# A two-block vision tower with a mixture of experts: slack in the order table, and ScalarE's squares in the last layer norm

## The reference, cut to what matters

```python
h = tok(x)                                   # gated projection
h = layernorm(h + attention_window(h))       # block 0, 16 heads, window of 64 each side
h = layernorm(h + quantised_mlp(h))          # block 0, the "quantised layer"
h = layernorm(h + attention_causal(h))       # block 1, 16 heads
h = layernorm(h + experts(h))                # block 1, 8 experts, top 2

# quantised_mlp: every input row is scaled to +-127 and rounded, weights to -1, 0, 1
act_quant(x) = clip(round(x * s), -128, 127) / s,  s = 127 / max|x|
g = act_quant(x) @ Wg ; u = act_quant(x) @ Wu
out = act_quant(square(relu(g)) * u) @ Wd

# experts: routing, capacity, two matmuls per expert, then a norm of its own
scores = softmax(x @ wg); gates, idx = top_k(scores, 2)
loc = cumsum(masks) - 1 + offsets;  keep = loc < C
y = layernorm(h + moe) * gamma + beta        # first norm of the end
out = layernorm(h + y)                       # second norm of the end
```

## Time and profile before

| | |
|---|---|
| median of 3 runs | 1016.46 us (1016.39 to 1018.25) |
| the profiled execution, its own time | 1015.96 us |
| its span, first to last instruction | 1014.1 us |
| first stage / experts / end | 0 to about 674 / to about 977 / to 1014.1 us |
| TensorE busy | 856.6 us (84%) |
| VectorE busy | 543.6 us (54%) |
| ScalarE busy | 415.4 us (41%) |
| GpSimd busy | 305.7 us (30%) |
| mean granted TensorE clock | 0.918 of full |

### The profile page before, as it was taken

The page is one execution under the profiler, slowest core; times in us unless marked ns, Lnnn a source line. Parts: engine busy times, 40 slices in busy tenths (PEclk is TensorE's granted clock), DMA queues, the critical chain, the costliest instruction groups (busy, mean ns, idle before and its releaser), DMA issues. The chain is left out here.

```text
span 1014.1 us, 14085 instructions
## 1 busy us (share of the span) xinstructions
PE 856.6 (84%) x4842; PEld 542.4 (53%) x4842; DVE 543.6 (54%) x2104; ACT 415.4 (41%) x717; POOL 305.7 (30%) x365
## 2 busy tenths in 40 slices
PE   6979999898697798798899798439999999999930
PEld 2655556556355345345445253326777877877820
DVE  1268535798798698788878685510211211210247
ACT  1316345585684576685565455113121021022003
POOL 6104214335244232122252422370213212311332
PEclk9999999899899799899799697659999999999975
DMA  9642202202202202202231300631135135233242
GB/s 347 201 180 65 65 21 64 64 3 64 64 2 64 64 1 64 64 1 64 85 105 33 97 1 26 248 120 42 16 125 141 21 120 141 46 100 68 29 106 83
DMA packets 57510, 81.48 MB, mean 80 GB/s; under 512 B 6624, under 2 KB 51041, under 8 KB 55008
## 3 DMA queue, kind: packets, MB, share of 16 engines
q1 hardware_dynamic: 49520, 70.48, 21.6%
q0 software_dynamic: 7296, 9.47, 5.5%
q10 hardware_dynamic: 624, 0.63, 0.2%
HBM read 35.37 MB, written 19.68 MB: 54 GB/s over the span
## 5 line engine op out<-in xcount | busy, mean ns | idle before, releaser
L1101 DVE CUSTOM_DVE_ANT_0 junk<-ps,maskb 128x256 bf16<-128x256 f32 (+4 forms) x512 | 205.4, 434 | 66.9 <-PE ps L820 63.1
L646 ACT ACTIVATE probs<-ps 128x512 f32<-128x512 f32 (+1 forms) x304 | 157.5, 551 | 93.1 <-PE ps L843 86.5
L1553 PE MATMUL ps<-dxT,qs 128*128 128x320 f32 x512 | 141.4, 437 | 1.3 <-DVE dxT L1617 1.3
L1565 PE MATMUL ps<-ks,hTe 128*128 128x256 f32 x640 | 139.3, 379 | 0.0
L1587 ACT ACTIVATE hTe<-ps,qs 128x640 f32<-128x640 f32 x64 | 50.8, 794 | 204.6 <-PE ps L1553 204.5
L1509 POOL DMA_INDIRECT mixed_rows<-ysb,ids x40 | 61.7, 1544 | 228.3 <-DVE ysb L1637 225.4
L1565 PEld LDWEIGHTS ps<-ks,hTe 128*128 128x128 f32 x640 | 121.1, 190 | 16.3
L843 PE MATMUL ps<-qs,ks 99*128 99x256 bf16 (+4 forms) x512 | 107.8, 298 | 21.4 <-DVE nmax L1101 8.8
L1553 PEld LDWEIGHTS ps<-dxT,qs 128*128 128x128 f32 x512 | 98.1, 192 | 42.6 <-DVE dxT L1617 1.9
L820 PE MATMUL ps<-ks,qs 96*128 96x256 bf16 (+4 forms) x512 | 107.8, 295 | 11.2 <-DVE nmax L1101 7.4
L859 PE MATMUL ps<-probs,vaug 128*32 128x256 f32 (+4 forms) x1024 | 93.7, 440 | 5.7 <-issue 4.2
(11 more groups left out here) (179 smaller groups left out, 1184.3 us busy)
## 6 DMA issues: line engine op xcount, KB each, us to landing
qs<-parts SPq DMA_DIRECT2D x96, 128.0 KB, 2.4
ks<-parts SPq DMA_DIRECT2D x96, 128.0 KB, 2.4
qs<-w SPq DMA_DIRECT2D x8, 1024.0 KB
ks<-w SPq DMA_DIRECT2D x8, 1024.0 KB, 4.9
dispatched_rows<-att SPq DMA_DIRECT2D x8, 650.0 KB, 10.5
ks<-dispatched_rows SPq DMA_DIRECT2D x4, 650.0 KB, 7.4
x_sb<-xT SPq DMA_DIRECT2D x8, 256.0 KB, 4.0
mixed_rows<-h SPq DMA_DIRECT2D x4, 512.0 KB, 3.6
```

Source lines behind the costliest of these rows:

```text
L646: act.activation(probs_of(u)[:, heads[0]:heads[-1] + 1, :], turned_bank((u, half, i))[:, 0:len(heads) * w].rearrange("p (j n) -> p j n", n=w),
L1101: ins = dve.tensor_tensor_reduce(out=junk[:, b - (b > V_BANK), a * (hi - lo):(a + 1) * (hi - lo)], in0=score_bank((u, half, i))[:, a * (hi ...
L1553: ins = mm(bank(2 * (n % 2) + c)[:, 0:HC], w1s[:, e % 2, k, m * P:(m + 1) * P], dxT[:, e % 2, k, c * HC:(c + 1) * HC], start=(k == 0), sto ...
L1565: ins = mm(bank(4 + n % 2)[:, 0:D], hTe[:, e % 2, m, t * P:(t + 1) * P], w2s[:, e % 2, m, :], start=(m == 0), stop=(m == MH - 1))
```

## The change

Five things are edited.

1. In "ffn" every piece from ScalarE's roundings on moves back by one: L759 from piece 0 to 1, L1278 from 1 to 2, the turn from 4 to 5 and the tiles from 5 to 6. The phase has 28 pieces and starts one step later for every batch. The tiles so stand two steps later than before.
2. In each tile ScalarE's rounding (L771) moves from the tile's step 2 to its step 3. VectorE's subtraction behind it stays in step 4.
3. Attention's norm (L1164) is cut in two: two tiles in piece 5, two in a new piece 6.
4. "route" gets an empty piece between the choice and the count: the count moves from piece 5 to 6, the positions from 6 to 8 to 7 to 9. The gate and route of batch 2 move from steps 249 and 251 to 258 and 260.
5. In the end, for batches 0 to 2, the second norm's statistics leave VectorE. The row sums come as a second output of the instruction that makes the input, a small instruction turns them into minus the mean, and ScalarE squares the centred rows and sums the squares as a second output. Batch 3 keeps the statistics as they were.

```diff
-    ("wq", 2, 20), ... ("o", 0, 54), ("ffn", 0, 60),
-    ("qkv", 3, 66), ("o", 1, 85), ("ffn", 1, 91), ...
+    ("wq", 2, 20), ... ("o", 0, 54), ("ffn", 0, 61),
+    ("qkv", 3, 66), ("o", 1, 85), ("ffn", 1, 92), ...
-    ("o", 6, 245), ("gate", 2, 249), ("route", 2, 251), ("send", 2, 271), ("o", 7, 278), ("gate", 3, 282),
+    ("o", 6, 245), ("gate", 2, 258), ("route", 2, 260), ("send", 2, 271), ("o", 7, 278), ("gate", 3, 282),
-STEPS = {"tok": 12, "qkv": 8, "o": 6, "ffn": 27, "gate": 2, "route": 9, ...}
+STEPS = {"tok": 12, "qkv": 8, "o": 7, "ffn": 28, "gate": 2, "route": 10, ...}
-FQT, FIRST_TILE, PER_TILE = 4, 5, 4
+FQT, FIRST_TILE, PER_TILE = 5, 6, 4
@@ scalar, ffn
-                            if c == 0:
+                            if c == 1:
                                 act.wait_ge(scale_done, i + 1)
...
-                            t = tile_at(c, HIDDEN + 1)
+                            t = tile_at(c, HIDDEN + 2)
                             if t is not None:
                                 act.wait_ge(fh_scaled, NT * i + t + 1)
@@ vector, quant
+                        if c == 2:
                             dve.wait_ge(fq_raised, NT * (i + 1))
@@ vector, o
-                            if c == 5:
-                                normed(0, NT, x, b, ROOTS["o", i])
+                            if c in (5, 6):
+                                normed(2 * (c - 5), 2 * (c - 5) + 2, x, b, ROOTS["o", i])
@@ scalar, the end
+                    def squares(q):
+                        act.wait_ge(mean2_done, q + 1)
+                        for t in range(q * NT, q * NT + NT):
+                            act.activation(n1[:, t, :], xa[:, t, :], ACT.Square, bias=nmean2[:, t:t + 1],
+                                           accum_out=sq2[:, t:t + 1]).then_inc(sq2_done, 1)
+
+                    squares(0)
                     for q in range(B):
-                        act.wait_ge(cbias[1], q + 1)
+                        if q + 1 < LAST:
+                            squares(q + 1)
+                        act.wait_ge(cbias, q + 1)
@@ vector, the end, second(q)
+                                dve.scalar_tensor_tensor(xa[:, t, :], n1[:, t, :], rs[:, 0, t:t + 1], hb(t), ALU.mult,
+                                                         ALU.add, accum_out=sum2[:, t:t + 1]).then_inc(xb_done, 1)
...
+                        if q:
+                            last_bias(q - 1)
+                        if q < LAST:
+                            dve.wait_ge(xb_done, q * NT + NT)
+                            dve.tensor_scalar(nmean2[:, c], sum2[:, c], -1.0 / D, None,
+                                              ALU.mult).then_inc(mean2_done, 1)
+                        else:
+                            stats(1, q)
+                    def variance(q):
+                        dve.wait_ge(sq2_done, q * NT + NT)
+                        dve.tensor_scalar(sq2[:, c], sq2[:, c], 1.0 / D, EPS_LN, ALU.mult, ALU.add).then_inc(cvar[1], 1)
...
                     for q in range(B):
                         if q + 1 < B:
                             begin(q + 1)
+                        if q:
+                            variance(q - 1)
                         second(q)
-                        if q:
-                            last_bias(q - 1)
```

More of the change, by code:

```diff
@@ L98 @@
     ("tok", 0, -20), ("qkv", 0, -8), ("tok", 1, -4), ("bias", 0, 1), ("bias", 1, 2), ("wq", 0, 4), ("wq", 1, 8),
-    ("wq", 2, 20), ("qkv", 1, 14), ("tok", 2, 22), ("tok", 3, 34), ("qkv", 2, 38), ("o", 0, 54), ("ffn", 0, 60),
-    ("qkv", 3, 66), ("o", 1, 85), ("ffn", 1, 91), ("qkv", 4, 98), ("o", 2, 117), ("ffn", 2, 123), ("qkv", 5, 130),
-    ("o", 3, 149), ("ffn", 3, 155), ("qkv", 6, 162), ("o", 4, 181), ("gate", 0, 185), ("route", 0, 187),
+    ("wq", 2, 20), ("qkv", 1, 14), ("tok", 2, 22), ("tok", 3, 34), ("qkv", 2, 38), ("o", 0, 54), ("ffn", 0, 61),
+    ("qkv", 3, 66), ("o", 1, 85), ("ffn", 1, 92), ("qkv", 4, 98), ("o", 2, 117), ("ffn", 2, 124), ("qkv", 5, 130),
+    ("o", 3, 149), ("ffn", 3, 156), ("qkv", 6, 162), ("o", 4, 181), ("gate", 0, 185), ("route", 0, 187),
     ("send", 0, 196), ("qkv", 7, 196), ("o", 5, 213), ("gate", 1, 217), ("route", 1, 219), ("send", 1, 228),
-    ("o", 6, 245), ("gate", 2, 249), ("route", 2, 251), ("send", 2, 271), ("o", 7, 278), ("gate", 3, 282),
+    ("o", 6, 245), ("gate", 2, 258), ("route", 2, 260), ("send", 2, 271), ("o", 7, 278), ("gate", 3, 282),
     ("route", 3, 284), ("send", 3, 293),)
-STEPS = {"tok": 12, "qkv": 8, "o": 6, "ffn": 27, "gate": 2, "route": 9, "send": 4, "bias": 2, "wq": 4}
-FQT, FIRST_TILE, PER_TILE = 4, 5, 4
+STEPS = {"tok": 12, "qkv": 8, "o": 7, "ffn": 28, "gate": 2, "route": 10, "send": 4, "bias": 2, "wq": 4}
+FQT, FIRST_TILE, PER_TILE = 5, 6, 4
 HIDDEN = 1
@@ L318, in build @@
         hb_done, n1_done, xb_done = (sem(n) for n in ("hb_done", "n1_done", "xb_done"))
-        c_stats, cvar, crstd, cbias, fin_done, out_done = (
-            [sem(f"{n}{i}") for i in range(2)] for n in ("c_stats", "cvar", "crstd", "cbias", "fin_done", "out_done"))
+        c_stats, cvar, crstd, fin_done, out_done = (
+            [sem(f"{n}{i}") for i in range(2)] for n in ("c_stats", "cvar", "crstd", "fin_done", "out_done"))
+        cbias, mean2_done, sq2_done = (sem(n) for n in ("cbias", "mean2_done", "sq2_done"))
         y_in = [sem(f"y_in{i}") for i in range(NTT // 2)]
@@ L1027, in dense @@
                                 ins.then_inc(d_full(("gate", i, "lg"))[0], 1)
-                        if phase == "route" and c == 5:
+                        if phase == "route" and c == 6:
                             pe.wait_ge(chosen, i + 1)
@@ L1457, in build @@
             moments2 = sb3("moments2", [P, NTT, 2])
+            sum2 = sb3("sum2", [P, NTT])
+            sq2 = sb3("sq2", [P, NTT])
+            nmean2 = sb3("nmean2", [P, NTT])
             rs = sb3("rs", [P, 2, NTT])
@@ L1678, in last_bias @@
                         dve.wait_ge(crstd[1], q + 1)
-                        dve.scalar_tensor_tensor(nb2[:, c], moments2[:, c, 0], -1.0, rs[:, 1, c], ALU.mult,
-                                                 ALU.mult).then_inc(cbias[1], 1)
+                        if q < LAST:
+                            dve.tensor_tensor(nb2[:, c], nmean2[:, c], rs[:, 1, c], ALU.mult).then_inc(cbias, 1)
+                        else:
+                            dve.scalar_tensor_tensor(nb2[:, c], moments2[:, c, 0], -1.0, rs[:, 1, c], ALU.mult,
+                                                     ALU.mult).then_inc(cbias, 1)
                     dve.wait_ge(hb_done, NTT)
```

30 lines of the change are left out of this document (17 added, 13 removed).

## The result

The changed kernel takes 999.79 us (median of 4 runs, 999.01 to 1000.09) against 1017.11 us for the kernel before beside it (4 runs, 1016.39 to 1018.25): a ratio of 0.9829, 95% interval 0.9805 to 0.9853. The forecast was 1007.0 us with 999 to 1018 around it. Faster was right, and 7 of the 17 us were not foreseen. The profiled execution took 999.01 us with a span of 997.1 us, 17.0 us less than before.

The account below looks back on a forecast made before the run. VectorE was taken to bound layer starts and the end, and with TensorE the quantised tiles. -4.2 - 3.4 - 1.8 = -9.4 us from 1015.96 gives 1006.6, plus 0.5 to the median 1007.0 us; forecast's own range 1002 to 1011, overall 999 to 1018.

Parts of the forecast that it names:

- What bounds the kernel: First stage: TensorE and VectorE both full in the quantised layer's tiles, VectorE alone at layer starts; the end is VectorE's chain.
- part 2: ScalarE's rounding L771 in each tile, one step later: not on the path, 0 us, between -2 and +12.
- Part 1: Roundings and start of the layer: VectorE's wait at L1278, four pieces, goes; -4.2 us, bounds 2.8 to 6.9.
- Part 3: Tiles two steps later: last tiles' statistics and norm move beside the next attention layer's sum; 0 us, between -4 and +7.
- the cut norm: Attention's norm cut in two at the layer's start: a bank comes free 1 us earlier, costed at nothing.
- Part 4: Routes: TensorE's waits around batch 2's route go, positions' delay hidden behind GpSimd's mask; -3.4 us, between -7 and +2.
- Part 5: The end: statistics of batches 0 to 2 leave VectorE, squares go to ScalarE; -1.8 us, between -3.4 and -0.5.
- The signs named ahead: Checks: L1280 under 1.5 us, no TensorE waits around 612 to 620 us, end 1.5 to 2 us shorter, L1707 wait.
- The clock: Rival: shorter stalls at layer starts and batch 2's route leave TensorE at full clock; 998 us, chance 0.16.
- Load, not waits: Rival: VectorE's bursts are only shifted and waits return later; only the end and about 1 us stay; 1013.5 us, chance 0.20.
- The late rounding: Rival: in the tiles L771 comes later and VectorE waits for it over sixteen gaps; 1018.5 us, chance 0.16.
- The squares set the end: Rival: if one ScalarE square takes 1.1 us, the end gives nothing and somewhat more; 1009.5 us, chance 0.06.

Follow-up runs that it names:

- part 4 alone: Kernel before with only batch 2's gate and route at 258 and 260 and the empty piece in every route: 1017.71 us, ratio 0.9989.
- the changed kernel timed again: The changed kernel, unaltered, timed a second time beside the leave-one-out kernels: 998.40 us, ratio 0.9817 to the kernel before.
- the ruler: Kernel before with only the end's edits (squares on ScalarE, accumulator outputs on VectorE), first stage untouched, so its trace serves as comparison there: 1016.42 us, ratio 0.9963.
- one step further: The changed kernel with L771 one step later still, in the step of VectorE's subtraction: 1023.81 us, ratio 1.0079 to the kernel before.

## Why the prediction was right in sign and short in size

- **What bounds the kernel, and part 2 (0 us): wrong, and the step that failed.** "This is not on the path, since VectorE is full in these tiles" rested on one window, 285.6 to 307.2 us, with VectorE at 20.71 of 21.60. Over steps 60 to 184 it is busy 243 of 291 us, and 22.1 of its idle us are at the maxima, waiting for TensorE. The prediction asked what the rounding itself delays (the subtraction, with room), and not what is queued behind the waiting rounding on ScalarE. Queued there was work that empties TensorE's banks (L665 in the tile shown): its waits for ScalarE fall from 20.3 to 6.6 us with part 2. That is worth 8.6 us alone and 14.3 in the changed kernel; the bound of -2 was far off.
- **Part 1 (-4.2):** the wait went as said (4.2 to 0.8), and in the changed kernel it is worth 3.9. Taken alone it is worth nothing that can be measured, and in its trace TensorE's longer busy time at a lower clock takes back the 6.6 us of idle time that it saved; a sum of separate terms could not say this.
- **Part 3 (0), and the cut norm (0, priced within part 1):** nothing can be measured for the cut norm. The later tiles have no run of their own; they are in part 1's, where ScalarE waits 6.3 us more at L771 (26.1 to 32.4).
- **Part 4 (-3.4):** the move gave 5.1, the clock among it; the empty piece took 3.0 where the prediction put nothing. "That wait is hidden behind the mask" was wrong by 0.9 to 1.1 us at GpSimd, and the cast queued behind it came late for VectorE; that this is the whole of the 3.0 is not shown. "The scatter of batch 2 stays at step 271" was true of the order and missed who waits behind it.
- **Part 5 (-1.8):** -3.0, inside its -0.5 to -3.4 and near the end at which both accumulator reads cost nothing. The mechanism was right, the prices too high: 1.98 us for the squares in place of 2.7, and next to nothing in place of 0.08 us for an accumulator output on VectorE.
- **The signs named ahead** came in the main: 0.8 us at L1280, no waits for the maxima's banks around the old 612 to 620 us, 2.14 us at L1707, the experts from 660 us on. The count waits 0.69 us where nothing was expected, the end is 3.0 us shorter and not 1.5 to 2, and the clock's mean is 0.922.
- **The rivals.** The clock did come along at batch 2's route (0.85 to 0.95 with part 4 alone); in the layers it is 0.92 in the profiled execution against 0.94 before, and 0.93 in the changed kernel timed again against 0.92 in the ruler, so the gain there is in the main not the clock's. "Load, not waits" (1013.5, by its own terms 1013.7) fell by the time, though half of its sign came: TensorE's waits for the maxima in steps 60 to 184 went only from 11.2 to 9.2 us, and what fell was its waits for ScalarE. "The late rounding" did not happen, but one step further it does. "The squares set the end" fell: four take 1.98 us (985.38 to 987.36).
- The Trainium skill (ScalarE: Activation LUTs, Rules for kernel authors) would keep adds and multiplies, which a square is, on VectorE. By the same page's figures (What ACT_TABLE_LOAD costs) four squares take an estimated 1.7 us; measured are 1.98 with their accumulator reads. On the price of the instructions this case agrees (1.79 us for four tiles' statistics on VectorE); the gain comes from taking work off the engine whose list is the chain.

Open: how much more the parts of the layer are worth together than apart, and why the clock is granted less with part 1 alone. By the ratios the parts come to -5.8 us apart (-8.6 + 1.7 + 1.1) and to -12.7 together, by the medians to -10.2 and -12.8, and each of these ratios is uncertain by 2 to 3 us. Leaving one out says that parts 1 and 2 help each other by some 4 to 6 us. The windows put most of that down to TensorE's busy time at the granted clock and not to more idle time saved; they are single traces, and two traces of the same instructions in this stretch differ by up to 3.5 us (290.8 before, 294.3 in the ruler).

## What to carry to other kernels

Price a wait by what is queued behind it on the waiting engine, and by who needs that: an engine busy two thirds of the time (ScalarE, 196 of 291 us) cost 9 to 14 us, because banks hung on it. Where an instruction between two engines has slack, move it until the wait is small on both sides, and no further: the first step later gained 14 us in the changed kernel, the second lost 25. Test edits to an order table alone and also by leaving each one out of the whole, and look at the granted clock beside the waits: in the traces part 1 saved about the same idle time either way, and it paid only with part 2 beside it. Slack in the order table is not free either: before an item is moved past a queue with long issues, read the list of that queue.
